# Two changes to a state-space and expert kernel: the side work in other slots, and the turned half sums added by TensorE and copied out by ScalarE

## The reference

```python
x = silu(_causal_depthwise_conv(x, conv_w, conv_b))
x_dbl = x @ x_proj_w.T
dt = softplus(x_dbl[..., :DT_RANK] @ dt_proj_w.T + dt_proj_b)
y = _selective_scan(x, dt, Bm, Cm, A, D)   # h = exp(dt*A)*h + dt*x*B ; y = sum_n C*h + D*x
y = y * silu(z)
...
return out_fwd + flip(out_rev)             # then @ out_proj_w.T, residual
```

## Time and profile before

| | us |
|---|---|
| median of 3 runs | 1510.51 |
| lowest, highest | 1504.71, 1515.46 |
| profiled execution | 1515.73 |
| its span | 1513.9 |

### The profile page before, as it was taken

One profiled execution on the slowest core, in us unless ns is written; L12 is line 12 of the kernel. 1 busy time (PEld: TensorE's weight loads), 2 busy tenths in 40 slices (PEclk: granted clock), 3 DMA queues, 4 the chain that ended last, 5 costly groups with the idle time before them and its releaser, 6 DMA issues. The chain is left out here.

```text
span 1513.9 us, 16479 instructions
## 1 busy us (share of the span) xinstructions
PE 1317.4 (87%) x5214; PEld 782.4 (52%) x5214; DVE 971.2 (64%) x1171; ACT 741.3 (49%) x1263; POOL 992.6 (66%) x518
## 2 busy tenths in 40 slices
PE   7589898899878877988967768788999999999997
PEld 3133333343223332432422223344899999999996
DVE  3488899999997898889989989894311111111110
ACT  3578866679674566875645664361111111111111
POOL 0489999999997897998989998780222222222221
PEclk9699999999997899999989889898899999999999
DMA  4335445454443444434444444432789898989892
GB/s 161 103 125 168 137 163 147 139 167 141 155 150 128 136 142 153 139 129 152 153 143 161 152 150 153 146 105 70 294 284 324 309 324 309 325 306 328 305 318 73
DMA packets 103144, 282.45 MB, mean 187 GB/s; under 512 B 9249, under 2 KB 19106, under 8 KB 87570
## 3 DMA queue, kind: packets, MB, share of 16 engines
q1 hardware_dynamic: 95570, 271.17, 51.9%
q0 software_dynamic: 7488, 10.23, 3.1%
HBM read 271.40 MB, written 9.96 MB: 186 GB/s over the span
## 5 line engine op out<-in xcount | busy, mean ns | idle before, releaser
L400 PE MATMUL ps_y<-arena,ident 128*128 128x512 f32 x1024 | 515.4, 638 | 89.0 <-POOL arena L1084 88.8
L1084 POOL TENSOR_TENSOR arena<-arena 128x1024 f32<-128x1024 f32 x192 | 453.6, 2367 | 63.3 <-DVE arena L834 40.6
L400 PEld LDWEIGHTS ps_y<-arena,ident 128*128 128x128 f32 x1024 | 196.6, 201 | 364.6 <-issue 209.0
L1070 POOL TENSOR_TENSOR arena<-arena 128x1024 f32<-128x1024 f32 x128 | 302.1, 2360 | 5.6 <-issue 4.1
L1118 POOL DMA_INDIRECT out_x<-arena x39 | 61.8, 1585 | 318.1 <-ACT arena L773 318.1
L648 ACT ACTIVATE ps_de<-arena,An 128x512 f32<-128x512 f32 x256 | 175.9, 687 | 161.2 <-DVE arena L831 160.1
L818 DVE TENSOR_TENSOR ps_u<-ps_du,arena 128x512 f32<-128x512 f32 x256 | 178.6, 698 | 23.8 <-DVE arena L845 8.0
L648 ACT ACTIVATE arena<-arena,An 128x512 f32<-128x512 f32 x256 | 181.2, 708 | 0.0
L1035 DVE TENSOR_TENSOR arena<-ps_du,arena 128x512 f32<-128x512 f32 x39 | 27.0, 691 | 231.9 <-PE ps_du L528 231.9
L831 DVE TENSOR_TENSOR_SCAN arena<-ps_de,arena 128x512 f32<-128x512 f32 x128 | 155.4, 1214 | 27.0 <-ACT arena L648 23.6
L831 DVE TENSOR_TENSOR_SCAN arena<-ps_de,hlast,arena 128x512 f32<-128x512 f32 x128 | 163.1, 1274 | 9.0 <-ACT arena L648 8.9
(11 more groups left out here) (221 smaller groups left out, 1555.1 us busy)
## 6 DMA issues: line engine op xcount, KB each, us to landing
arena<-bc_scratch SPq DMA_DIRECT2D x256, 512.0 KB, 4.6
arena<-in_W SPq DMA_DIRECT2D x117, 1024.0 KB, 8.2
arena<-in_xT SPq DMA_DIRECT2D x2, 1024.0 KB, 6.4
arena<-in_w2c SPq DMA_DIRECT2D x1, 2048.0 KB, 9.2
arena<-in_xT SPq DMA_DIRECT2D x4, 512.0 KB, 6.3
X_scratch<-stg SPq DMA_DIRECT2D x12, 128.0 KB, 4.5
out_x<-stg SPq DMA_DIRECT2D x12, 128.0 KB, 4.8
ipT<-in_ipT SPq DMA_DIRECT2D x1, 1024.0 KB, 7.6
```

The lines of the kernel that those rows point to most:

```text
L400: t = e.matmul(Y[j][:, :], ident[:, :], hc[:, i % NP, j, :], start=False, stop=(n == 15))
L1070: e.tensor_tensor(uA[:, turn % 2, :, :], duA.rearrange("p (o t) -> p o t", o=1).to_broadcast([128, 2, TH]), ring[:, turn % NR, 0, :, :], A ...
L1084: e.tensor_tensor(hc[:, i % NP, :, :], hh[:, i % NH, :, :], c, ALU.mult).then_inc(gp_hc, 1)
```

## The change

The tables of slots are written anew. Most readers on ScalarE come one slot later (a silu in slot +3 and no longer +2, and so on), two gates are taken by ScalarE in one slot, the output block is split over two slots of TensorE, the logits are read one slot earlier by VectorE, and the tiles of batch 0 move by some 64 slots. `flip` is gone: in a backward pass TensorE adds the forward pass's sum out of `ya` into Y at n = 5 and 6 of each group by one more identity product for each bank, and ScalarE's `evac` copies Y, read backwards, to `ya` in all 16 groups, in slot +4 (EV). Since every copy turns the time axis once, both passes meet in the same order. The last two gates are made behind the last unit, in the banks of the decays.

```diff
-NR, ND, NH, NP, KD, LAG, NW = 3, 3, 3, 3, 6, 2, 3
+NR, ND, NH, NP, KD, LAG, EV, NW = 3, 3, 3, 3, 6, 2, 4, 3
...
-CONV_FROM, ROWS_FROM = [14, 2, 14], [38, 28, 38]
...
+STEP_AT = {1: (0, 0, 1), 16: (0, 1, 0), 33: (0, 1, 1), 41: (1, 0, 0), 62: (1, 0, 1),
...
+CONV_SLOTS = {1: (4, 8, 12, 19, 21, 24, 27, 30),
...
-GATE_AT = {at(1, 34): (0, 1, 0), at(1, 36): (0, 1, 1), at(1, 38): (0, 1, 2), at(1, 40): (0, 1, 3),
+GATE_AT = {at(1, 42): (0, 1, 0), at(1, 43): (0, 1, 1), at(1, 47): (0, 1, 2), at(1, 48): (0, 1, 3),
...
-OUT_AT = {at(1, 45): (0, 1, 0), at(1, 46): (0, 1, 1), at(2, 12): (0, 0, 0), at(2, 13): (0, 0, 1),
+OUT_AT = {at(1, 53): (0, 1, 0), at(1, 54): (0, 1, 1), at(2, 14): (0, 0, 0), at(2, 15): (0, 0, 1),
...
-TILE_AT = {at(1, 48): (0, 4), at(1, 52): (0, 5), at(1, 57): (0, 6), at(1, 62): (0, 7),
-           at(2, 43): (0, 0), at(2, 47): (0, 1), at(2, 52): (0, 2), at(2, 58): (0, 3),
-           at(3, 44): (1, 4), at(3, 47): (1, 5), at(3, 50): (1, 6), at(3, 53): (1, 7)}
+TILE_AT = {at(2, 46): (0, 4), at(2, 50): (0, 5), at(2, 58): (0, 6), at(2, 62): (0, 7),
+           at(3, 2): (0, 0), at(3, 6): (0, 1), at(3, 14): (0, 2), at(3, 18): (0, 3),
+           at(3, 44): (1, 4), at(3, 48): (1, 5), at(3, 52): (1, 6), at(3, 56): (1, 7)}
...
+                    if n == 5 + j and q % 2:
+                        e.wait_ge(ac_ev, nth_sum(q - 1, 1 - th, m))
+                        e.matmul(Y[j][:, :], ident[:, :], ya[:, m, cols_of(q, th)], start=False, stop=False)
...
                 if i in OUT_AT:
-                    out_block(*OUT_AT[i], side)
+                    out_block(*OUT_AT[i], side, (0, 1))
+                if i - 1 in OUT_AT:
+                    out_block(*OUT_AT[i - 1], side, (2, 3))
...
+                else:
+                    e.wait_ge(dv_sA, i - 1)
+                    gate(*LAST_GATES[i - NU], [4 + i - NU])
...
-                    e.activation(ya[:, 2 * pr + j, HB[th]], Y[j][:, :], ACT.Copy).then_inc(ac_ev, 1)
+                    e.activation(ya[:, 2 * pr + j, cols_of(q, th)], Y[j][:, ::-1], ACT.Copy).then_inc(ac_ev, 1)
...
-                if i > LAG and (i - LAG - 1) % 16 == 15 and unit(i - LAG - 1)[0] % 2 == 0:
-                    evac(i - LAG - 1)
+                if i >= EV and (i - EV) % 16 == 15:
+                    evac(i - EV)
...
-            def flip(i):
-                q, th, pr, n = unit(i)
-                e.wait_ge(pe_y, i + 1)
-                for m in (2 * pr, 2 * pr + 1):
-                    e.wait_ge(ac_ev, nth_sum(q, 1, m))
-                    half = ya[:, m, cols_of(q, th)]
-                    e.tensor_tensor(half, half, Y[m % 2][:, ::-1], ALU.add).then_inc(dv_fl, 1)
```

162 lines of the change are left out of this document (81 added, 81 removed).

## The result

The changed kernel took **1461.1 us** (median of 4 runs, 1459.92 to 1461.22) against 1510.3 for the kernel before beside it (median of 4, 1504.71 to 1515.46): ratio 0.967, 95% interval 0.964 to 0.971. Run once more, it took 1464.7 (1459.1 to 1465.3), ratio 0.969 [0.964, 0.973]. The prediction was 1474 with a range from 1462 to 1495: faster, as foretold, and 13 us more so, just outside the range; the second median, 1464.7, lies inside it.

What follows compares the result with a forecast made beforehand. GpSimd and VectorE were taken as two full engines, stalled where TensorE waits for side banks. Floors of 915.1 plus 4 us gave 919.1 against 958.2, 39 less; together 41 less than 1515.7: 1474 us, range 1462 to 1495.

Steps and rivals of the forecast that it cites:

- the count of takings: 22 takings of banks 6, 7 under two slots behind VectorE's reading: halves four 5, five 5, six 3, eight 9.
- TensorE full: Rival, 12%: convolutions and identity products make TensorE lag, GpSimd waits; three halves at 4 to 5 us each, 1488.
- ScalarE too late: Rival, 4%: ScalarE's waits and copies at group ends hold up the scans; 1543, or 1509 if half do.
- it doesn't do what it says: Rival, 8%: bank waits are an effect of TensorE at half clock, so only the flips' waits go; 1495.
- the floor for each half: For each 32-unit stretch between VectorE's scans, the larger of GpSimd's busy time and VectorE's chain; eight sum to 915.1 us.
- the 4 us on top: Half a us for each of the eight halves, for waits that stay; 919.1 us in all.
- Half eight, 117.0: VectorE's chain of 110.4 us plus 3 gates and 2 blocks (3.4) and 4 tiles (3.2).
- Half five, 114.0: VectorE 107.0 + 4.0 = 111.0 us, GpSimd busy 113.5; taken as 114.0.
- Half one, 119.5: GpSimd 113.0 us; first units wait for ScalarE (idle 10.0), of which wider slots take perhaps a third.
- Half seven, 111.5: VectorE's chain of 107.0 us plus 4 tiles, moved here from batch 0, and 2 gates (4.5).
- The estimate from below: Halves lose VectorE's idle time above half two's and seven flips: about 907 us, 51 less; as a rival 1463, 7%.
- The end: Last two gates wait only for scans and stand before the last adds; with the x reload, 2 us less.

Runs made afterwards that it cites:

- tables_only: The changed kernel's new slots and readers, but with the turned sums added by VectorE in flip as in the kernel before; 1474.2 us, ratio 0.976.
- before_light: The kernel before with the silu left out of the 24 convolutions, so that ScalarE needs fewer table loads; 1502.6 us, ratio 0.995.
- best: The changed kernel plus idle router products, the last gate behind the last add and 15 idle identity products ahead of the first slot; 1463.6 us, ratio 0.972.
- after_again: The changed kernel run once more with nothing altered; 1464.7 us, ratio 0.969 against the kernel before.

## Why the prediction missed its range

**What held.** The places: halves four, five, six and eight, named by the count of takings, gave 16.1, 17.5, 5.1 and 9.6 us, 48.2 of the 48.8. That is so only because the other four cancel (−6.2, +2.9, −0.5, +3.2); halves two and seven grew by more than the "up to 2" foretold, and half five ended a us under its 112 to 119. The first step of the mechanism held as well: TensorE's waits for VectorE's readings went from 49.3 us to 0.2. GpSimd idles 2.5 us behind adds (under 4 foretold) and 10.4 behind scans (under 25). The copies cost little in slot +4 (the scans' waits for ScalarE are 2.9 us with them and 1.2 without, in tables_only), and more in slot +3. TensorE isn't full: 102.5 of 113.1 us in half three. The rivals "TensorE full", "ScalarE too late" and "it doesn't do what it says" are out. On ScalarE's table loads the trace stays with its 0.02 us behind a load: half five ran in 111.0 us at 83.6 busy.

**The step that failed: the floor for each half and the 4 us on top.** The sum of floors was 915.1, 919.1 with the residual; measured were 909.4, and 907.0 in the same kernel's second profile. The terms:

- The 4 us "for waits that stay": the halves came out under the sum of floors even with all their waits, so −4.
- Half eight, 117.0: measured 113.6. It ends with its last scan, so it holds one input L822, seven own products and 31 inputs of a unit (L833, 0.70 us each), and I had counted two, eight and 32: 2.9 us of the 3.4.
- Half five, 114.0: measured 111.0. I had taken GpSimd's busy time in the window of before (113.5, 56 instructions) as its floor. It isn't one of that half alone: GpSimd's work moves over a window's edge (108.5 us and 54 instructions after, while half six rose from 108.9 to 113.1). Over all eight it was 881 us before and 880 after. A sum of eight maxima lies above the largest of the two sums, and that bias was all on one side.
- Half one, 119.5: measured 116.8. I let a third of the idle time at the start go; tables_only, with 115.4, shows that the scans' waits for ScalarE go nearly whole (15.0 us there before, 0.4 in tables_only).
- Half seven, 111.5: measured 113.9, and 111.9 in the second profile, so that no cost of its tiles above their 0.8 us is shown.

With halves two (3.0 too low), four (1.4 too high) and the small ones, −9.7 in all. In the second profile two and four come out at 112.9 and 114.4, so what stands in both are the 4 us and halves one, five and eight. Together with the start (−0.8), the end (+2.4), the router (−5.2) and 0.3 elsewhere that is the distance from 1474.7 to 1461.1.

The estimate from below, about 907, had the number right and stood in the text as a rival with 7%. It did so partly by luck: done as it is described, each half never under GpSimd's busy time, it gives 900; 907 comes out only with half one's 119.5 from the list of floors in place of its 113.0.

**The causes were read too narrowly.** The waits of scans for ScalarE, 32.5 us, served only as an argument for a rival, that copies would add to them. They were part of the gain: the new rows take nearly all of them. before_light removed a third of them for 7 us of the time, by taking 45 loads from ScalarE, where the change takes 14. What part of the changed kernel's gain is theirs and not the banks' can't be parted, since the same rows do both.

**The end.** Foretold −2, measured +0.4. I took the gate before the last add for the reason; best moved it behind and gained nothing there (13.2 us), so why the end is no shorter stays open.

**The router's clock.** Not in the sum at all: 5.2 us in this profile. It would account for the step from the 1464.7 of after_again to 1461, and so out of the range; only one execution of each was profiled, so for the others that is argued and not shown. A range whose low end is a sum without any such swing was too narrow by some 5 us on that side.

**The base.** I subtracted from a profiled execution 5 us above its median. By the medians the change gave 48 to 49 us, not 41; taken from the median the same 41 us give 1469.5.

## What to carry to other kernels

A list of close takings of a shared bank finds the places that are crowded, but not the price of one: put into a table with room, four or twelve of them were absorbed. What a repair gives in a crowded place depends on what else stands there: moving four tiles was enough for half four (13.3 us), while in half five no partial repair brought it under 122, and the new rows for all engines brought it to 115.0. A sum of the fullest engine's work over each part, with a residual on top, was 10 us too long here, and the fullest engine's work over the whole (881 us of GpSimd, with 909 measured) 28 too short; give the range room for both, and an estimate from below a real chance when the stalls' cause is removed everywhere. A wait that is large in the profile (32.5 us here) is to be asked whether the change removes it, not only whether it adds to it. And profile the same kernel more than once before a us or two in one part is read as an effect.
